# Second FFN of a macaron block: row normalization of the last blocks inside the mixer's pipeline, and row scatters issued in pairs that wait for the scatters ahead

## Chip, cores and metric

The kernel runs on one core of one Trainium2 chip. The metric is the device time of one launch in microseconds (us), lower is better. The engines are PE (TensorE, matmuls), DVE (VectorE), ACT (ScalarE), POOL (GpSimd) and SP (SyncE, which only issues DMAs here). Each engine runs its own list of instructions in order, and they wait for one another by semaphores.

## What is computed

The input x has 4 sequences of 1024 tokens with 128 features. Cut to its frame, the reference is

```python
x = x + 0.5 * ffn(layernorm(x))       # first FFN: shared + 2 of 8 experts per token
x = x + attn(layernorm(x))            # state space mixer with its own small FFN
x = x + 0.5 * ffn(layernorm(x))       # second FFN, same weights as the first

def ffn(x):
    shared = (silu(x @ sw1) * (x @ sw2)) @ sw3
    probs = softmax(x @ rw + rb); w, idx = top_k(probs, 2); w = w / sum(w)
    routed = sum over the 2 chosen experts e of w * ((silu(x @ ew1[e]) * (x @ ew2[e])) @ ew3[e])
    return shared + routed
```

## The kernel before

The 4096 tokens are 8 blocks (`NB`) of 512 tokens, each of 4 tiles of 128. The program has three phases: first FFN, mixer, second FFN. An FFN runs as follows for each block: statistics of x (`dve_stats`, L1374 and L1378), the power -0.5 of the variance on POOL (`pool_rstd`, L694 and L696), the normalized rows (`dve_norm`, L1390, four instructions), transposes on PE, router logits, the two chosen experts (`dve_route`, L1398 to L1420), a rank of every token within its expert (`pe_rank`, L1967 to L1971) and from it the row of a table in HBM where the token goes (`dve_places`, L1427 to L1437, whose last step increments `pos_ready`). `pool_scatter` (L703) then sends the rows of the block to the table `xs`: 8 indirect DMAs, one for each tile and each of the two chosen experts, each of 128 rows of 520 bytes. Each DMA adds 16 to the semaphore `scattered` when it has landed.

Beside the routing runs the shared FFN, two halves per block: `pe_up` (L1980 and L1982), silu on ACT (L1001), the product on DVE (`dve_hid`, L1474), `pe_down` (L1990) and the addition into x (`dve_shared`, L1479). Then SP loads tiles of 128 rows of one expert from `xs` (L458). It does so when all scatters have landed and when the last `pe_up` is done (L451), since the loads overwrite a buffer that `pe_up` reads. PE transposes these tiles (L2003), multiplies them with the expert's weights (L2016 to L2042), and POOL scatters the answers to `ys` (L719). At last DVE adds the answers to x (`dve_combine`, L1525).

The mixer is a software pipeline. `in_order` calls a body for n = -8 to 16, and each step in the body works on block n + k with a k of its own; the order of calls in the four bodies is the order of instructions on the engines. A block leaves the mixer with `ffn_add` (L1310, which increments `mixer_done`), and blocks 0 to 4 (`EARLY` = 5) go on in the same pipeline through the routing of the second FFN: `route_stats`, `route_rstd`, `route_rows`, `route_choice`, `route_places`, and the eight scatters of the block in four pairs (`route_scatter` 0 to 3). Blocks 5 to 7 are routed after the mixer, in `dve_ffn_again`, `pe_ffn_again` and `pool_ffn`. There DVE first takes the statistics and rows of the three blocks, then goes through the turns of the shared FFN with the routing of one late block in each of the first three turns. In the first FFN and after the mixer, POOL issues the 8 scatters of a block one behind the other with no wait between them.

Of the kernel before, what the change touches and what calls it, by code (L numbers as in the profile page):

```python
# [16 lines left out]
NB = TOK // BT  # L17
TT = BT // P
# [11 lines left out]
EARLY = 5  # L30
# [5 lines left out]
SQ = SEQ // BT  # L36
# [52 lines left out]
def macaron(nc, A, out):  # L89
    ctx = ExitStack()  # L90
    with ctx:
# [209 lines left out]
        scattered = sem("scattered")  # L301
# [80 lines left out]
        def do(work, block, *which):  # L382
            if block:
                work(*block, *which)

        def early(block):
            return block if block and SQ * block[0] + block[1] < EARLY else None

        def in_order(body):

            for n in range(-8, NB + 9):
                body(lambda k: (((n + k) // SQ, (n + k) % SQ) if 0 <= n + k < NB else None))
# [10 lines left out]
        block = ctx.enter_context(nc.Block())  # L403
# [101 lines left out]
        def pool_mixer(pool, ffn_own):  # L505
# [138 lines left out]
            def body(at):  # L644
# [3 lines left out]
                do(route_scatter, early(at(-9)), 0)  # L648
                do(route_rstd, early(at(-7)))
                do(route_scatter, early(at(-9)), 1)  # L650
# [47 lines left out]
        def pool_scatter(pool, turn, which=range(2 * TT)):  # L698

            n = turn % NB  # L700
            pool.wait_ge(pos_ready, turn + 1)
            for i in which:
                pool.indirect_dma_start(xs, bass.IndirectOffsetOnAxis(pos[:, n, i:i + 1], 0),  # L703
                                        rows[:, n * TT + i % TT, :], None).then_inc(scattered, 16)
# [18 lines left out]
        def pool_ffn(pool, own, call):  # L723
# [12 lines left out]
            else:  # L736

                for n in range(EARLY, NB):
                    pool_rstd(pool, own, NB + n)
                for n in range(EARLY, NB):  # L740
# [348 lines left out]
        def dve_mixer(dve, combine, ffn_own):  # L1089
# [238 lines left out]
            def body(at):  # L1328
                do(b_between, at(-4))
                do(route_stats, early(at(-7)))  # L1330
                do(ffn_hidden, at(-6), 0)
# [4 lines left out]
                do(stats_of, at(3))  # L1336
                do(route_rows, early(at(-7)))
                do(gram_copy, at(-4), 0)
# [240 lines left out]
        def dve_ffn_again(dve, own):  # L1579
            dve.wait_ge(mixer_done, NB)  # L1580
            late = range(EARLY, NB)
            for n in late:
                dve_stats(dve, own, NB + n)
            for n in late:
                dve_norm(dve, NB + n)
            for n in range(NB + 1):
# [5 lines left out]
                if n < NB:  # L1592
                    dve_hid(dve, NB + n, 1)
                if n:
                    dve_shared(dve, NB + n - 1)
# [590 lines left out]
```

## Time and profile before

| | us |
|---|---|
| median of 3 runs | 859.64 |
| lowest and highest run | 859.44, 863.35 |
| the profiled execution, own time | 859.07 |
| its span | 857.3 |
| share of the chain of waits put down to no engine of the profile | 15% |
| first FFN, to the first addition of its answers (L1525) | 0 to 266.9 |
| mixer, to the end of the last L1310 | 266.9 to 624.3 |
| second FFN, shared part and routing | 624.3 to 697.4 |
| second FFN, experts | 697.4 to 836 |
| last additions and stores | 836 to 857 |

A row of a timeline gives start, duration, engine, line, operation, output and inputs, how many instructions it merges, and in brackets the idle time of that engine just before and what ended it. The name "remote", and in the chain of waits "another core or an unknown queue", stands where the engine waited and the work on which it waited ended well before, so that the profile knows no releaser; there is only one core here.

### The profile page before, as it was taken

What the parts mean: (1) busy time and instruction counts of PE and PEld (TensorE: products, weight loads), DVE (VectorE), ACT (ScalarE), POOL (GpSimd) and SP (SyncE); (2) the same over time, 40 slices, a digit from 0 to 9 for tenths busy, and PEclk for the clock granted to TensorE, in tenths of its full rate; (3) what the DMA queues carried; (4) which work ended last, traced back from release to release, by engine and by line L of the source; (5) the groups of instructions that cost most, each with busy time, mean ns of one, the idle gap of its engine ahead of it and who ended that gap; (6) DMA issues with size and microseconds to landing.
All of it is one profiled execution on the core that took longest, in us unless ns stands there. A gap on an engine that the chain in (4) does not pass through costs nothing.

```text
span 857.3 us, 13671 instructions
## 1 busy us (share of the span) xinstructions
PE 659.9 (77%) x3768; PEld 481.7 (56%) x3768; DVE 543.7 (63%) x1730; ACT 413.1 (48%) x713; POOL 518.4 (60%) x656
## 2 busy tenths in 40 slices
PE   2448489888970557989999998989788689898840
PEld 2325258777760225656676665757555468686730
DVE  5535355544535787897999999997363445445518
ACT  1212124444430899997999998552121124344410
POOL 3875573555554675896978878767736105565550
PEclk9977889999995869889999998999979799999975
DMA  9311123222214100000000000000101122222218
GB/s 269 126 51 35 40 70 78 67 73 72 80 39 156 41 0 1 1 2 1 1 2 1 1 14 16 10 23 27 37 14 50 40 51 77 70 76 71 62 47 268
DMA packets 55512, 46.34 MB, mean 54 GB/s; under 512 B 8456, under 2 KB 51053, under 8 KB 55440
## 3 DMA queue, kind: packets, MB, share of 16 engines
q1 hardware_dynamic: 46736, 28.54, 12.2%
q0 software_dynamic: 8704, 16.93, 6.0%
q8 instruction: 34, 0.56, 0.3%
q14 instruction: 38, 0.31, 0.1%
HBM read 25.30 MB, written 21.19 MB: 54 GB/s over the span
## 4 chain that ended last, share of the span: by engine, by line
PE 42%; DVE 19%; another core or an unknown queue 15%; ACT 10%; issue 9%; POOL 3%; DMA 2%; DVEq 0%; POOLq 0%; ACTq 0%; SPq 0%
PE ps_tr L1640 3%; PE ps_tr L2042 3%; PE ps_go L2029 3%; PE ps_go L1640 2%; DVE x L1525 2%; PE ps_a L1980 2%; PE ps_b L1982 2%; PE ps_go L1990 2%; PE ps_go L2042 2%; PE ps_a L2018 2%; PE ps_go L1811 1%; PE ps_tr L1828 1%; ACT arena L1030 1%; PE ps_a L2016 1%
## 5 line engine op out<-in xcount | busy, mean ns | idle before, releaser
L719 POOL DMA_INDIRECT ys<-arena,dest x144 | 140.8, 978 | 154.5 <-DVE arena L1517 91.6
L703 POOL DMA_INDIRECT xs<-rows,pos x128 | 126.0, 984 | 67.7 <-issue 35.3
L2029 PE MATMUL ps_go<-ident,hid 128*128 128x128 f32 x288 | 44.3, 277 | 26.5 <-ACT arena L1030 18.0
L1001 ACT ACTIVATE silu_a<-ps_a 128x512 f32<-128x512 f32 x32 | 19.0, 597 | 94.3 <-remote 46.5
L2029 PEld LDWEIGHTS ps_go<-ident,hid 128*128 128x128 f32 x288 | 34.4, 142 | 41.8 <-issue 33.0
L1030 ACT ACTIVATE arena<-ps_go 128x512 f32<-128x512 f32 x72 | 43.0, 597 | 27.6 <-remote 21.8
L2042 PE MATMUL ps_tr<-w_down_e,arena 128*128 x384 | 52.4, 281 | 0.0
L1507 DVE TENSOR_TENSOR hid<-silu_a,ps_b 128x512 f32<-128x512 f32 x36 | 24.7, 685 | 38.6 <-issue 31.2
L2042 PEld LDWEIGHTS ps_tr<-w_down_e,arena 128*128 128x128 f32 x384 | 48.2, 197 | 0.0
L1990 PEld LDWEIGHTS ps_go<-w_shared_down,hid 128*128 128x128 f32 x256 | 34.7, 213 | 16.2 <-issue 16.0
L1507 DVE TENSOR_TENSOR hid<-silu_a,ps_a 128x512 f32<-128x512 f32 x36 | 24.6, 685 | 28.7 <-issue 16.3
L1021 ACT ACTIVATE silu_a<-ps_b 128x512 f32<-128x512 f32 x36 | 21.5, 598 | 43.0 <-remote 21.3
L1990 PE MATMUL ps_go<-w_shared_down,hid 128*128 128x128 f32 x256 | 35.1, 295 | 9.0 <-DVE x L1479 9.0
L1474 DVE TENSOR_TENSOR hid<-silu_a,ps_b 128x512 f32<-128x512 f32 x32 | 21.9, 686 | 29.9 <-PE ps_b L1982 15.7
L1517 DVE COPY arena<-ps_tr 128x256 f32<-128x256 f32 x48 | 20.3, 423 | 29.8 <-remote 24.4
L1479 DVE TENSOR_TENSOR x<-x,ps_go 128x512 f32<-128x512 f32 x16 | 11.0, 686 | 43.8 <-remote 30.3
L1811 PE MATMUL ps_go<-arena,state 128*128 128x128 f32 x128 | 32.2, 336 | 8.2 <-DVE us L1277 6.9
L1013 ACT ACTIVATE xt_hi<-ps_tr 128x256 fp32r<-128x256 f32 x48 | 18.5, 385 | 39.9 <-PE ps_tr L2003 25.6
L1021 ACT ACTIVATE silu_a<-ps_a 128x512 f32<-128x512 f32 x36 | 21.6, 600 | 32.9 <-PE ps_a L2018 18.0
L2016 PE MATMUL ps_a<-up_hi,xt_hi 128*128 x72 | 31.5, 438 | 5.2 <-DVE xt_lo L1492 3.8
L1941 PE MATMUL ps_tr<-ident,rows 128*128 128x128 f32 x64 | 14.0, 358 | 26.8 <-DVE rows L1390 19.8
L1811 PEld LDWEIGHTS ps_go<-arena,state 128*128 128x128 f32 x128 | 22.2, 207 | 20.4 <-issue 13.9
(366 smaller groups left out, 2053.0 us busy)
## 6 DMA issues: line engine op xcount, KB each, us to landing
arena<-xs SPq DMA_DIRECT2D x144, 65.0 KB
rows<-ys SPq DMA_DIRECT2D x8, 512.0 KB, 4.0
arena<-ys SPq DMA_DIRECT2D x8, 512.0 KB, 7.7
ys<-arena,dest POOLq DMA_INDIRECT x144
x<-in_L_attn_x SPq DMA_DIRECT2D x8, 256.0 KB, 4.4
arena<-in_L_ffn_ew SPq DMA_DIRECT2D x4, 512.0 KB, 6.3
xs<-rows,pos POOLq DMA_INDIRECT x128
out<-x SPq DMA_DIRECT2D x8, 256.0 KB, 3.8
```

The lines of the kernel that those rows point to most:

```text
L703: pool.indirect_dma_start(xs, bass.IndirectOffsetOnAxis(pos[:, n, i:i + 1], 0), rows[:, n * TT + i % TT, :], None).then_inc(scattered, 16)
L719: pool.indirect_dma_start(ys, bass.IndirectOffsetOnAxis(dest[:, i:i + 1], 0), y_out[:, p % YRING, j, :], None, bounds_check=2 * TOK - 1, o ...
L1021: act.activation(silu_a[:, p % 2, :].rearrange("p (j h) -> p j h", j=2), ps_pair[p % 2][:, :, 0:HID], ACT.Silu).then_inc(silu_e_done, 1)
L1030: act.activation(hid_t[:, p % 2, :], ps_d, ACT.Copy).then_inc(ht_ready, 1)
L1474: dve.tensor_tensor(hid[:, turn % 2, k, :], silu_a[:, k, :], ps_b[:, k, :], ALU.mult).then_inc(hid_done, 1)
L1507: dve.tensor_tensor(hid[:, p % 2, 0, :].rearrange("p (j h) -> p j h", j=2), silu_a[:, p % 2, :].rearrange("p (j h) -> p j h", j=2), ps_pai ...
L1640: r = pe.matmul(target, weights(k), zt[:, shift:shift + BT], start=(k == 0), stop=(k == taps - 1))
L1811: pe.matmul(pb["o"][:, at], state[:, k % 2, p * P:(p + 1) * P], cfs[:, q, k * P:(k + 1) * P], start=True, stop=False)
L1990: r = pe.matmul(ps_d[:, t * P:(t + 1) * P], hid[:, turn % 2, k, t * P:(t + 1) * P], w_shared_down[:, k, :], start=(k == 0), stop=(k == 1))
L2016: pe.matmul(target, xt_hi[:, p % 2, mine], hi, start=True, stop=False)
L2029: r = pe.transpose(ps_d[:, at:at + P], hid[:, p % 2, 0, at:at + P], ident[:, :])
L2042: r = pe.matmul(ps_answers(p)[:, j * P:(j + 1) * P], hid_t[:, p % 2, at:at + P], w_down_e[:, bass.ds(which[2 * p + j], 1), k, :].rearrange ...
```

## The change

Three things change in the second FFN, none in the first.

- `route_stats` and `route_rstd` in the mixer's pipeline are called for all 8 blocks, and `route_rows` for all but the last. The work for blocks 5 to 7 at the head of `dve_ffn_again` and `pool_ffn` is gone; the rows of block 7 are made after the two products of the first turn.
- `pool_scatter`, when it works for the second FFN (`turn >= NB`), waits before every second scatter until all scatters ahead have landed. This holds for the 40 scatters in the mixer's pipeline and for the 24 after it.
- Logits, choices, ranks and places of blocks 5 to 7 stay where they are.

```diff
@@ macaron
+        def not_last(block):
+            return block if block and SQ * block[0] + block[1] < NB - 1 else None
@@ pool_mixer, body
                 do(route_scatter, early(at(-9)), 0)
-                do(route_rstd, early(at(-7)))
+                do(route_rstd, at(-7))
                 do(route_scatter, early(at(-9)), 1)
@@ pool_scatter
             n = turn % NB
             pool.wait_ge(pos_ready, turn + 1)
             for i in which:
+                if turn >= NB and i % 2 == 0:
+                    pool.wait_ge(scattered, 16 * (turn * 2 * TT + i))
                 pool.indirect_dma_start(xs, bass.IndirectOffsetOnAxis(pos[:, n, i:i + 1], 0),
@@ pool_ffn
-                for n in range(EARLY, NB):
-                    pool_rstd(pool, own, NB + n)
                 for n in range(EARLY, NB):
                     pool_scatter(pool, NB + n)
@@ dve_mixer, body
-                do(route_stats, early(at(-7)))
+                do(route_stats, at(-7))
...
-                do(route_rows, early(at(-7)))
+                do(route_rows, not_last(at(-7)))
@@ dve_ffn_again
             dve.wait_ge(mixer_done, NB)
-            late = range(EARLY, NB)
-            for n in late:
-                dve_stats(dve, own, NB + n)
-            for n in late:
-                dve_norm(dve, NB + n)
...
                     dve_hid(dve, NB + n, 1)
+                if n == 0:
+                    dve_norm(dve, NB + NB - 1)
```

POOL at the end of the mixer's pipeline, from the addition of the last block's h to x. Before, where `scattered` is not waited for:

```order
L623 TENSOR_TENSOR x<-x,arena 128x512 [waits m_hmv]
...
L703 DMA xs<-rows,pos 33920x130 [waits pos_ready]
L703 DMA xs<-rows,pos 33920x130
L703 DMA xs<-rows,pos 33920x130 [waits pos_ready]
L703 DMA xs<-rows,pos 33920x130
L694 TENSOR_SCALAR var_eps<-mv 128x4 [waits mv_ready]
L696 TENSOR_TENSOR rstd<-var_eps,minus_half 128x4 [waits own_pool]
```

After, from the same instruction on:

```order
L626 TENSOR_TENSOR x<-x,arena 128x512 [waits m_hmv]
L709 DMA xs<-rows,pos 33920x130 [waits scattered,pos_ready]
L709 DMA xs<-rows,pos 33920x130
L709 DMA xs<-rows,pos 33920x130 [waits scattered,pos_ready]
L709 DMA xs<-rows,pos 33920x130
L709 DMA xs<-rows,pos 33920x130 [waits scattered,pos_ready]
L709 DMA xs<-rows,pos 33920x130
L697 TENSOR_SCALAR var_eps<-mv 128x4 [waits mv_ready]
L699 TENSOR_TENSOR rstd<-var_eps,minus_half 128x4 [waits own_pool]
L709 DMA xs<-rows,pos 33920x130 [waits scattered,pos_ready]
...
```

Before, six pairs stand in a row and the three L694/L696 of blocks 5 to 7 come behind them. Now the power for block 6 stands behind the third pair, that of block 7 behind the sixth (that of block 5 is between pairs one step earlier), and each pair waits for `scattered`.

DVE at the end of the mixer and the start of the second FFN. Before:

```order
L1304 TENSOR_TENSOR arena<-arena,ps_b 96x512 [waits m_silu_g,m_up_ps]
L1310 TENSOR_TENSOR x<-x,ps_tr 128x512 [waits m_h_added,m_ffn_ps]
L1374 BN_STATS stats<-x 128x6 [waits m_mixer_done]
...
L1390 TENSOR_SCALAR rows<-x,mv,rstd 128x128 [waits rstd_ready,mv_ready]
L1390 TENSOR_SCALAR rows<-x,mv,rstd 128x128 x3
L1474 TENSOR_TENSOR hid<-silu_a,ps_b 128x512 [waits down_ps_ready,b_ps_ready,silu_done] x2
L1398 TENSOR_TENSOR logits<-ps_tr,rb 128x32 [waits logits_ps_ready]
```

After:

```order
L1308 TENSOR_TENSOR arena<-arena,ps_b 96x512 [waits m_silu_g,m_up_ps]
L1394 TENSOR_SCALAR rows<-x,mv,rstd 128x128 [waits rstd_ready,mv_ready]
L1394 TENSOR_SCALAR rows<-x,mv,rstd 128x128 x3
L1314 TENSOR_TENSOR x<-x,ps_tr 128x512 [waits m_h_added,m_ffn_ps]
L1378 BN_STATS stats<-x 128x6 [waits m_mixer_done]
...
L1478 TENSOR_TENSOR hid<-silu_a,ps_b 128x512 [waits b_ps_ready,down_ps_ready,silu_done,m_mixer_done]
L1478 TENSOR_TENSOR hid<-silu_a,ps_b 128x512 [waits down_ps_ready,b_ps_ready,silu_done]
L1394 TENSOR_SCALAR rows<-x,mv,rstd 128x128 [waits rstd_ready,mv_ready]
L1394 TENSOR_SCALAR rows<-x,mv,rstd 128x128 x3
L1402 TENSOR_TENSOR logits<-ps_tr,rb 128x32 [waits logits_ps_ready]
```

The rows of block 6 now stand ahead of the last `ffn_add`, which lets PE start the second FFN. Twelve statistics and twelve row instructions ahead of the first product become four statistics, and the rows of block 7 stand between the second product and the first late choice.

## Rows read from the trace of the kernel before

**Rows 1.** Chain of waits, 580 to 700 us: start, length, what; the unknown pieces.

```profile
588.38 2.24 another core or an unknown queue
...
614.45 9.13 another core or an unknown queue
...
657.09 12.83 another core or an unknown queue
```

**Rows 2.** Timelines by engine, end of the mixer, 606 to 624 us.

```profile
606.50 1.07 POOL L703 DMA_INDIRECT xs<-rows,pos  x1 [0.17 <-issue]
...
620.51 0.96 POOL L703 DMA_INDIRECT xs<-rows,pos  x1 [0.30 <-issue]
...
615.15 2.94 PE L1875 MATMUL ps_tr<-w_down,arena 128*128 128x128 f32 x24 [0.78 <-issue]
...
623.61 0.69 DVE L1310 TENSOR_TENSOR x<-x,ps_tr 128x512 f32<-128x512 f32 x1 [8.51 <-remote]
```

**Rows 3.** Timeline, second FFN, 644 to 672 us.

```profile
644.60 0.24 PE L1971 MATMUL ps_go<-chosen,ones 128*128 128x8 bf16 x4
...
648.85 0.19 DVE L1427 TENSOR_TENSOR place<-ps_go,base 128x32 f32<-128x32 f32 x1 [3.89 <-remote]
...
656.95 2.69 PE L1990 MATMUL ps_go<-w_shared_down,hid 128*128 128x128 f32 x16
...
668.96 0.96 POOL L703 DMA_INDIRECT xs<-rows,pos  x1 [0.30 <-issue]
669.94 0.69 DVE L1479 TENSOR_TENSOR x<-x,ps_go 128x512 f32<-128x512 f32 x1 [12.85 <-remote]
```

**Rows 4.** Timelines, mixer: scatters in pairs, with PE and ACT beside them.

```profile
558.59 0.96 POOL L703 DMA_INDIRECT xs<-rows,pos  x1 [0.30 <-issue]
...
559.38 0.27 PE L1745 MATMUL ps_a<-ident,bf 128*128 128x128 f32 x1
...
559.69 0.49 ACT L913 ACTIVATE tm<-ps_a 128x384 f32<-128x384 f32 x1 [6.37 <-PE ps_b L1788]
...
561.39 1.00 POOL L703 DMA_INDIRECT xs<-rows,pos  x1 [0.17 <-issue]
```

**Rows 5.** DMA, 606 to 624 us: all queues that moved anything.

```profile
q0 software_dynamic: 384, 0.80, 13.5%
```

**Rows 6.** Timeline by engine: head of the second FFN, DVE, then POOL.

```profile
627.87 3.23 DVE L1390 TENSOR_SCALAR rows<-x,mv,rstd 128x128 f32<-128x128 f32 x12
631.01 0.68 DVE L1474 TENSOR_TENSOR hid<-silu_a,ps_b 128x512 f32<-128x512 f32 x1
...
637.60 0.17 DVE L1437 CAST pos<-pos_f 128x8 uint32<-128x8 f32 x1
...
626.03 1.04 POOL L696 TENSOR_TENSOR rstd<-var_eps,minus_half 128x4 f32<-128x4 f32 x1
...
638.06 1.10 POOL L703 DMA_INDIRECT xs<-rows,pos  x1 [8.19 <-DVE pos L1437]
```

**Rows 7.** Chain of waits: the last answer scatter, from its issue to its landing.

```profile
830.22 2.11 DMA ys<-arena,dest
```

**Rows 8.** SP's waits, and timeline 684 to 706 us.

```profile
SPq L451 <- PE ps_b L1982: 14.8, 1, 14.8
...
692.24 13.27 SPq L458 DMA_DIRECT2D arena<-xs  x16
...
697.47 0.44 PE L2003 MATMUL ps_tr<-ident,arena 128*128 128x128 f32 x2 [0.78 <-DVE x L1479]
```

**Rows 9.** Window: stretch, length, busy of PE, PEld, DVE, ACT, POOL, granted clock, DMA, GB/s.

```profile
621.00:624.00 3.00, 0.00 (x0) 0.00 (x0) 0.40 (x1) 0.00 (x0) 0.47 (x1) 0.50 0.07 22
```

**Rows 10.** Chain of waits: matmuls of the shared FFN.

```profile
629.03 1.71 PE ps_b L1982 x2
...
686.79 1.78 PE ps_go L1990 x16
...
690.29 0.86 PE ps_a L1980 x2
```

## The prediction

> **What bounds the kernel now.** I read the chain of waits first. Of 857.3 us it puts 15% down to no engine, and three of these pieces lie where the change works: 2.2 us at 588, 9.1 us at 614 and 12.8 us at 657 [rows 1]. The timelines of the engines say what stands there. At the end of the mixer PE ends its last `down` at 618.09 (615.15 + 2.94), but the DVE addition that needs only that starts at 623.61, 5.5 us late [rows 2]. In the second FFN a rank matmul ends at 644.84 and DVE uses it at 648.85, 4.0 us late. A `pe_down` ends at 659.64 and DVE uses it at 669.94, 10.3 us late, and all other work of the shared FFN queues up behind [rows 3]. A long idle time whose releaser had been done for long means that the news of PE's end came late, not that an engine was slow. So what else ran? In each case POOL was issuing scatters back to back: 12 of them from 606.50, one each 1.26 us (0.96 busy, 0.30 of issue), the last at 620.51 [rows 2], and 16 up to 668.96 [rows 3]. The engines wake up 1 to 3 us after the start of the last one. Where only two scatters stand together and POOL then does something else, nothing is late: with one running, PE ends at 559.65 and ACT starts at 559.69; the next pair starts 1.8 us after the last one's end [rows 4].
>
> My reading is that PE's increments of semaphores are held up while POOL scatters without a pause, and pass when it pauses. That is inferred from coincidence in time; the trace has no row for the path itself.
>
> The Trainium skill (Runtime: NRT & Kernel Launch, section on instruction fetch mechanics) names another thing that can stop several engines without a releaser: instructions are streamed in blocks of 16 KiB by DMA. By this, stalls would go with instruction packets and the change would not touch them. The trace speaks against it: from 606 to 624 us only the software queue moved anything, 384 packets [rows 5].
>
> **The waits in `pool_scatter`.** A pair takes 1.26 to 1.40 us from first to second start (0.96 + 0.30; the first after other work is 1.10 or 1.07 long [rows 2, 6]), then its landing, then the release of POOL. The landing of an indirect DMA has one clean row, 2.11 us from issue [rows 7]. A release is 0.29 us, from the end of the cast at 637.77 to the scatter at 638.06 [rows 6]. Together 3.66 to 3.80; I take 3.75 us for a pair, where it was 2.52. Between the end of the second and the next start POOL pauses 1.4 us, close to the 1.8 us that were enough in [rows 4]. In the steady mixer most pairs already stand farther apart, so the wait is met when POOL comes to it. At 588 one pair follows another and waits 1.1 us, behind it is a product for the last block that is needed later.
>
> **End of the mixer.** The power of block 5 (1.4 us: 1.04 [rows 6] and a short instruction ahead) and one wait push POOL's train of six pairs from 606.5 to about 607.2. Behind the third pair (607.2 + 2 x 3.75 + 1.40 + 0.96 = 617.1) stands the power of block 6, done at 618.4. DVE waits for it with the rows of block 6 (3.23 / 3 = 1.1 us [rows 6]) **ahead of the last `ffn_add`**, which is thus free at 619.6. That is a new wait, but without the hold `ffn_add` could start at 618.1 at best. Against 623.61 the mixer ends 4.0 us earlier. The three remaining pairs run behind that, to about 628, and the power of block 7 comes at 629.6.
>
> **Head of the second FFN.** Removed in front of the first product are 8 of 12 statistics and all 12 row instructions. This looks like 6 us, but PE's `ps_b` for that product ended at 630.74 [rows 10] and DVE took it at 631.01 [rows 6], so the removal is worth 0.3 us. What is added is the rows of block 7 (1.1 us) between the second product and the choice of block 5. Places and scatters of block 5 move by -4.0 + 1.1: the first late scatter goes from 638.06 to 635.2.
>
> **Shared FFN.** From the rank matmul at 644.84 on, PE still has 11 halves of up (2 x 0.86 = 1.72) and 7 downs (1.78 [rows 10]), 31.4 us. I add 3 us for transposes and logits and 2.5 us for waits on DVE, both estimates: an end at 681.7 without any hold, where the trace has 697.4 with the last addition. Moved by -2.9 it is 678.8.
>
> **Scatters after the mixer.** Twelve pairs: 635.2 + 11 x 3.75 + 1.26 + 2.11 = 679.8. Before, this end was of no matter, since SP waited 14.8 us for the last up of PE [rows 8]. Now it is the later of the two, by a microsecond against the end of the shared FFN, by 6 against the last up. SP starts loading tiles at 679.9 instead of 692.24.
>
> **Start of the experts.** Before, PE started on the tiles 5.2 us after SP, held by the last addition. Now it is the loads themselves: 2.1 us of landing as in [rows 7] at least, 5.2 at most; I take 2.9, hence 682.8 instead of 697.47, 14.7 us earlier. Something is given back. PE is idle from about 678 on, and after such a stop the clock was granted at half (0.50 in 621 to 624, PE having stopped at 618 [rows 9]), the level of 1.2 GHz; two ups still took 1.71 us at 629 where they take 0.86 [rows 10]. That can cost 0 to 3.5 us of the experts; I take 2.5. The experts and the last additions are otherwise unchanged.
>
> **Sum.** Against the profiled execution of 859.07: -14.7 + 2.5 = -12.2, so 846.9. The median of the runs is 0.57 above it: 847.4 us.
>
> **Rivals.**
>
> - *Hold only in part gone.* A post may still be late within a pair. At some 0.4 us on each of three handoffs in eight turns, the shared FFN ends 10 us later (689) and binds again: 697.4 - 689 = 8.4 earlier, 851. A pair cadence of 4.2 us, with the fills of SP on the same DMA engines, gives 11 x 0.45 = 5 us later, 852. For it: the pause is shorter than in [rows 4]. Chance 0.20.
> - *No link.* The engines stall for another reason and as long as before, and the waits only make POOL's train longer. Then `ffn_add` and the end of the shared FFN stay, and the last landing (638.06 + 1.1 + 44.7 = 683.9) is before SP's 692.2: about 860. The Trainium skill (DMA: Bandwidth & Descriptors, rules for kernel authors) advises to issue DMAs early and wait late, since the fixed cost then overlaps, and this change does the reverse. By that rule alone it could not gain, and would come out here. Against it: every long stall lies on a train of scatters. Chance 0.07.
> - *Slower: the hold lasts for the train, pauses or not.* If 1.4 us are too little, posts wait until the train ends. The mixer's train ends near 630 instead of 623.6 (+6.4), and the late one, begun 7.5 us later, lasts 44.7 us to 690.3 where it ended near 671. Everything behind moves by 19 us: 878. It decides at the pause that a post needs, which is above 0 and, by [rows 4], at most 1.8. Chance 0.08.
> - *Main case*, 843 to 850. Chance 0.60. The last 0.05 is faster than that: both trains shorter (3.66 us a pair) and no loss of clock, down to 842.
> - That the edit does not do what it says is excluded by the order of instructions.
>
> **How the numbers follow.** The forecast is 847.4. The range 842 to 858 holds the main case with its bounds (cadence -1 to +0.6 us, load 2.1 to 5.2, clock 0 to 3.5) and the partial hold; it leaves out the two last rivals and a little more. A measurement can tell 0.5%, 4.3 us, from no change. Faster by more than that: 0.78. Within: 0.10. Slower: 0.12. Of the partial hold 0.13 counts as faster, 0.03 as within and 0.04, a hold of a larger size than the one priced, as slower.
>
> **What would show it.** Right: the last `ffn_add` starts within 0.2 us of the rows of block 6, near 619.6; no idle time of "remote" over 2 us until the tiles; scatters in pairs 3.7 us apart; SP's wait before the first tile ends with a landing, not with PE; a dip of the clock at the first tiles. Wrong: an idle time of DVE or ACT that still ends with the last scatter of a train; SP still waiting for PE; POOL's train so late that the power of block 7 holds the choice of block 5.

## The result

The changed kernel takes 853.2 us against 859.3 us (medians of 20 runs each), a ratio of 0.9942 with a 95% interval of 0.9919 to 0.9964. Faster, as forecast, but by 0.6% and not by the 1.4% that 847.4 us would have been: half of the gain did not come. One profiled execution of it has a span of 854.3 us, where the kernel before had 857.3.

The pieces without a releaser [rows 1] are gone between 480 and 700 us. What stands there in the chain of waits of the changed kernel (start, length, what) is POOL and the landings of its pairs:

```profile
by line: DMA xs<-rows,pos 45.9%; POOL xs L709 17.1%; issue 12.5%; DMA arena<-xs 4.8%; PE ps_a L2017 2.7%; SPq L461 2.0%; PE ps_a L2018 1.9%; PE ps_a L2019 1.9%; PE ps_b L2017 1.9%; PE ps_go L2004 1.6%; DVE hid L1478 1.5%; DVE top_i L1411 1.
...
612.87 2.28 DMA xs<-rows,pos
...
615.19 0.73 issue
615.92 0.96 POOL xs L709
...
661.56 0.27 issue
661.83 0.96 POOL xs L709
662.79 0.30 issue
663.09 3.02 DMA xs<-rows,pos
...
683.59 3.74 DMA xs<-rows,pos
...
691.34 0.35 SPq L461
```

(The first line has the shares of the stretch 655 to 700 us alone.) The timelines of the same kernel, answering to [rows 2], [rows 6] and [rows 8]: PE's last `down`, the rows of block 6 and the last `ffn_add`, the rows of block 7, the first late scatter, the last addition of the shared FFN, and PE's first tile.

```profile
617.86 2.94 PE L1876 MATMUL ps_tr<-w_down,arena 128*128 128x128 f32 x24 [0.78 <-DVE arena L1308]
...
624.00 1.12 DVE L1394 TENSOR_SCALAR rows<-x,mv,rstd 128x128 f32<-128x128 f32 x4 [6.20 <-POOL rstd L699]
625.03 0.68 DVE L1314 TENSOR_TENSOR x<-x,ps_tr 128x512 f32<-128x512 f32 x1
...
637.09 1.12 DVE L1394 TENSOR_SCALAR rows<-x,mv,rstd 128x128 f32<-128x128 f32 x4 [1.72 <-POOL rstd L699]
...
641.89 1.09 POOL L709 DMA_INDIRECT xs<-rows,pos  x1 [4.90 <-DVE pos L1441]
...
686.15 0.69 DVE L1483 TENSOR_TENSOR x<-x,ps_go 128x512 f32<-128x512 f32 x1 [2.21 <-PE ps_go L1991]
...
693.29 1.01 PE L2004 MATMUL ps_tr<-ident,arena 128*128 128x128 f32 x2 [7.17 <-DMA arena<-xs]
```

These times have to be read with a shift. One `hid` product of the mixer, long before anything that the change touches, starts at 472.04 in the kernel before and at 476.76 in the changed one:

```profile
472.04 1.76 DVE hid L1164
```

```profile
476.76 1.77 DVE hid L1168
```

So this execution of the changed kernel was 4.7 us late when the changed part began. With 4.7 us taken off, its first tile comes at 688.6 where it was at 697.47 [rows 8]: 8.9 us earlier, of a forecast 14.7.

### The profile page after: what moved, and what is told of

It reads as the page before. It is cut to its first block, busy times and chain, and to the rows that moved or that the text cites. A ratio compares the mean times of both kernels' runs of the same rounds, so it can differ in the third digit from the quotient of the medians.

```text
span 854.3 us, 13695 instructions
## 1 busy us (share of the span) xinstructions
PE 655.6 (77%) x3768; PEld 476.1 (56%) x3768; DVE 544.2 (64%) x1730; ACT 413.7 (48%) x713; POOL 519.3 (61%) x656
## 4 chain that ended last, share of the span: by engine, by line
PE 35%; another core or an unknown queue 14%; DVE 14%; issue 13%; ACT 9%; POOL 7%; DMA 6%; SPq 0%; POOLq 0%; DVEq 0%; ACTq 0%
DMA xs<-rows,pos 4%; POOL xs L709 4%; PE ps_tr L1641 4%; PE ps_go L1641 3%; PE ps_tr L2043 2%; PE ps_go L2030 2%; DVE x L1529 2%; ACT arena L1034 2%; PE ps_a L2019 2%; PE ps_go L1812 1%; PE ps_go L1816 1%; PE ps_go L1991 1%; PE ps_tr L1829 1%; PE ps_a L1981 1%
## 5 line engine op out<-in xcount | busy, mean ns | idle before, releaser
L1991 PEld LDWEIGHTS ps_go<-w_shared_down,hid 128*128 128x128 f32 x256 | 30.9, 193 | 7.2 <-issue 7.2
L2017 PE MATMUL ps_b<-up_hi,xt_hi 128*128 x72 | 32.2, 447 | 1.1 <-DVE xt_lo L1496 0.9
L1991 PE MATMUL ps_go<-w_shared_down,hid 128*128 128x128 f32 x256 | 31.5, 276 | 1.7 <-DVE x L1483 1.7
```

The source lines that it names most:

```text
L1991: r = pe.matmul(ps_d[:, t * P:(t + 1) * P], hid[:, turn % 2, k, t * P:(t + 1) * P], w_shared_down[:, k, :], start=(k == 0), stop=(k == 1))
L2017: pe.matmul(target, xt_hi[:, p % 2, mine], hi, start=True, stop=False)
```

## Experiments: two kinds of sessions

One thing must be told first. The kernels ran in several sessions (the texts written ahead of each run say "call"), each with runs of the kernel before on the same chip. In some sessions the median of the kernel before is 852 to 859 us, as in the first comparison; in others it is 781.8 to 782.7. Nothing lies between. y_before shows what is different.

**y_before** is the kernel before, unchanged.

> The kernel before, unchanged, for its trace beside the next ones. In the runs of the first comparison it took 859 us and its chain held pieces without a releaser; in the runs of moves-only and its three companions it took 783, and their traces have no such piece over 1.5 us although POOL scatters 12 and 24 in a row. Theory 'place' (whether the hold occurs depends on the chip or the process, not on the kernel): either some 782 us with no such piece, or some 859 with them, nothing in between. Rival 'luck within a run': a time between, with some of the pieces.

It took 782.1 us. By engine, the chain of its page has no unknown piece at all, where the kernel before had 15% in the first comparison. In the timelines, the last of twelve scatters starts at 584.60, and `ffn_add` follows the last `down` (end 582.20) without delay though the tenth is running; 24 late scatters run in a row up to 625.37, and the additions of the shared FFN are on time.

```profile
PE 49%; POOL 17%; DVE 13%; issue 10%; ACT 7%; DMA 2%; POOLq 0%; SPq 0%; DVEq 0%; ACTq 0%
```

```profile
579.26 2.94 PE L1875 MATMUL ps_tr<-w_down,arena 128*128 128x128 f32 x24 [0.78 <-DVE arena L1304]
...
582.24 0.69 DVE L1310 TENSOR_TENSOR x<-x,ps_tr 128x512 f32<-128x512 f32 x1 [3.04 <-PE ps_tr L1875]
...
584.60 0.96 POOL L703 DMA_INDIRECT xs<-rows,pos  x1 [0.30 <-issue]
...
595.77 1.10 POOL L703 DMA_INDIRECT xs<-rows,pos  x1 [6.09 <-DVE pos L1437]
...
640.83 0.44 PE L2003 MATMUL ps_tr<-ident,arena 128*128 128x128 f32 x2 [0.78 <-DVE x L1479]
```

So the hold, that is, news of PE's end that comes late while POOL scatters, is not a property of the kernel. It needs the scatters and something else that some sessions have. The chip's number does not tell it: sessions with the hold had the numbers 2, 3, 6, 8 and 14, those without 0, 6 and 8. What it is stays open. The loading of instructions does not explain it: both traces of the kernel before have the same 34 and 38 packets on the two instruction queues, and none of them moved from 640 to 650 us, where news was held.

Of the 77 us between the two traces of the kernel before, 42.3 lie before the first late scatter, and 35.6 of these before the mixer's first scatter (491.74 against 456.10), where the change does nothing. The part from the first late scatter to the first tile has 14.3 (59.4 against 45.1), the experts and what follows them 20.2 (159.8 against 139.6). So the change works on the smaller part of what the hold costs.

All comparisons, each against the kernel before in its own session, with the 95% interval:

| kernel | no hold | with the hold |
|---|---|---|
| changed kernel | 1.0173 (1.0144 to 1.0203) | 0.9942 (0.9919 to 0.9964) |
| moves only | 0.9976 (0.9959 to 0.9994), 0.9977 (0.9961 to 0.9993), 0.9989 (0.9974 to 1.0005) | 0.9947 (0.9906 to 0.9988) |
| waits only | 1.0230 (1.0200 to 1.0260) | |
| waits after the mixer only | 1.0068 (1.0045 to 1.0090) | |
| one wait a pair | | 0.9931 (0.9897 to 0.9965) |
| one wait, power first | 1.0306 (1.0262 to 1.0349) | |
| short pause, no wait | 0.9973 (0.9949 to 0.9996), 0.9960 (0.9938 to 0.9983) | 0.9938 (0.9898 to 0.9979) |
| fours | 1.0017 (0.9999 to 1.0034), 1.0027 (1.0012 to 1.0042) | |
| eights after the mixer | | 0.9836 (0.9810 to 0.9862) |
| fours after the mixer | | **0.9744** (0.9653 to 0.9835), **0.9784** (0.9742 to 0.9827) |

## Experiments: the parts of the change

**y_after** is the changed kernel, unchanged.

> The changed kernel, unchanged. Theory 'place': if the kernel before takes 859 us here, 853; if it takes 783 us, there is no hold to cure and only the price of the waits is left. Waits after the mixer alone were 788.8 (ratio 1.0068); with the pairs of 4.3 us in the mixer and the powers behind them the first late scatter comes some 4 to 5 us later still: 792 to 796 us, ratio 1.012 to 1.017, a slower kernel. Rival: the change is worth its 6 us everywhere, ratio 0.992 to 0.996.

795.1 us, ratio 1.0173: where there is no hold the change costs 1.7%, at the upper end of what "place" gave.

**x_moves_only, w_moves_only, v_moves_only, u_moves_only**, the changed kernel without the waits:

```diff
             for i in which:
-                if turn >= NB and i % 2 == 0:
-
-                    pool.wait_ge(scattered, 16 * (turn * 2 * TT + i))
                 pool.indirect_dma_start(xs, bass.IndirectOffsetOnAxis(pos[:, n, i:i + 1], 0),
```

> The changed kernel without the waits of the scatter pairs: only the statistics, powers and rows of blocks 5 to 7 are moved into the mixer's pipeline, and POOL scatters back to back as before. Theory 'hold' (PE's increments are late while POOL scatters without a pause, and the waits cure it): the idle pieces without a releaser come back at the end of the mixer (some 5 us between the end of the last down and the last ffn_add) and in the second FFN (4 and 10 us or more), SP again waits for the last up and not for a landing, and the time is that of before, 857 to 861 us (ratio to before 0.998 to 1.002). Rival 'moves' (the gain of 6 us comes from the moved rows): 852 to 854 us, ratio 0.992 to 0.995, with the stalls in place.

> The kernel of x_moves_only again (the moved statistics, powers and rows, without any wait for landings), for a call in which the hold shows. Where it does not, this kernel was 1.9 us faster than the kernel before (0.9976), while the changed kernel was 1.7% slower. Theory 'hold': the pieces without a releaser stand at the mixer's end and in the second FFN as in the kernel before, ratio 0.996 to 1.002. Rival 'the moves bring the gain': 0.990 to 0.995, no slower than the changed kernel.

> The kernel of x_moves_only once more; the question is what it does where the hold shows (kernel before some 855 to 860 us). Theory 'hold': its chain of waits has again pieces without a releaser of several us in the mixer's end and in the second FFN, and its ratio is 0.996 to 1.002, against 0.9942 of the changed kernel. Rival 'the moves bring the gain': 0.990 to 0.995. If the call falls where the kernel before takes 782 us: 0.9976 for the third time.

> The kernel of the moves-only runs once more, for a call in which the hold shows. v_pause_short fell into such a call: no piece without a releaser at the mixer's end, where the moved powers part the scatters into groups of six, but three in the second FFN (1.6, 1.9 and 10.6 us) that end 2.1 us after the last of 16 scatters. Theory 'a train of more than some six scatters holds until it has landed': without any pause the same: nothing or under 2 us at the mixer's end, 8 to 15 us in the second FFN, ratio 0.992 to 0.998. Rival 'the short pauses did it at the mixer's end': 5 us late there as in the kernel before, ratio 0.998 to 1.002.

The first three fell where there is no hold and gave 781.3, 781.0 and 780.8 us: the moved rows are worth 1 to 2 us by themselves there, and the waits cost 1.9%, some 14 us (795.1 against 781). The fourth had the hold, and my main theory, that the waits bring the gain, fell with it: 0.9947 (0.9906 to 0.9988), within the intervals as good as the changed kernel, without one wait. Its timeline shows two different things. At the end of the mixer nothing is late any more: the last `down` ends at 621.13 and `ffn_add` starts at 621.36, though twelve scatters run there as before. They are now six, the power of block 6, and six. In the second FFN the hold is there as before. The rank matmul ends at 642.03, 0.4 us into the sixth scatter, and DVE uses it at 645.15; ACT wakes at 646.58, after the eighth, and DVE again after the next eight.

```profile
618.19 2.94 PE L1873 MATMUL ps_tr<-w_down,arena 128*128 128x128 f32 x24 [0.78 <-DVE arena L1305]
...
617.84 0.95 POOL L706 DMA_INDIRECT xs<-rows,pos  x1 [0.31 <-issue]
618.82 0.27 POOL L697 TENSOR_SCALAR var_eps<-mv 128x4 f32<-128x4 f32 x1
619.17 1.04 POOL L699 TENSOR_TENSOR rstd<-var_eps,minus_half 128x4 f32<-128x4 f32 x1
620.41 1.09 POOL L706 DMA_INDIRECT xs<-rows,pos  x1 [0.20 <-issue]
...
621.36 0.68 DVE L1311 TENSOR_TENSOR x<-x,ps_tr 128x512 f32<-128x512 f32 x1
...
641.79 0.24 PE L1969 MATMUL ps_go<-chosen,ones 128*128 128x8 bf16 x4
...
644.18 0.96 POOL L706 DMA_INDIRECT xs<-rows,pos  x1 [0.30 <-issue]
...
645.15 0.19 DVE L1428 TENSOR_TENSOR place<-ps_go,base 128x32 f32<-128x32 f32 x1 [3.00 <-issue]
...
646.58 0.60 ACT L1002 ACTIVATE silu_a<-ps_a 128x512 f32<-128x512 f32 x1 [4.93 <-remote]
...
655.18 0.95 POOL L706 DMA_INDIRECT xs<-rows,pos  x1 [0.30 <-issue]
...
658.00 0.69 DVE L1480 TENSOR_TENSOR x<-x,ps_go 128x512 f32<-128x512 f32 x1 [9.95 <-remote]
```

**x_waits_only**, the kernel before plus those waits alone.

```diff
             for i in which:
+                if turn >= NB and i % 2 == 0:
+                    pool.wait_ge(scattered, 16 * (turn * 2 * TT + i))
                 pool.indirect_dma_start(xs, bass.IndirectOffsetOnAxis(pos[:, n, i:i + 1], 0),
```

> The kernel before plus only the waits of the scatter pairs; statistics, powers and rows of blocks 5 to 7 stay after the mixer. Theory 'hold': no idle piece without a releaser over 2 us, but the three powers now stand behind a POOL train that ends near 632 (six pairs of 4.3 us from 606.5), so that the rows and with them the first late scatter come near 646 where the changed kernel (its first 480 us being those of before) has 637. The late train of 49 us follows: some 5 to 9 us later than the changed kernel, 857 to 862 us. Rival 'waits alone bring it, moves are neutral': 852 to 854 us.

No hold in its session, and 802.7 us, 20 more than the kernel before. The reason is the one given: the three powers stand behind a train whose last scatter starts at 594.29 (584.60 in y_before), and the first late scatter starts at 609.76 after POOL has waited 10.4 us for DVE, where y_before has 595.77.

```profile
594.29 0.96 POOL L706 DMA_INDIRECT xs<-rows,pos  x1 [0.30 <-issue]
...
598.32 1.05 POOL L696 TENSOR_TENSOR rstd<-var_eps,minus_half 128x4 f32<-128x4 f32 x1
609.76 1.10 POOL L706 DMA_INDIRECT xs<-rows,pos  x1 [10.38 <-DVE pos L1440]
```

**x_waits_late**, the changed kernel with waits after the mixer only.

```diff
-                if turn >= NB and i % 2 == 0:
+                if turn >= NB + EARLY and i % 2 == 0:
```

> The changed kernel with the waits only in turns 13 to 15, that is for the twelve pairs after the mixer; the pairs in the mixer run without. Theory 'hold, each train for itself': the last ffn_add is again 5 us late behind the mixer's train, but the powers of blocks 6 and 7 no longer stand behind pairs of 4.3 us, which costs the changed kernel 2 us before the first late scatter and some more of the mixer's end. Together 0 to 3 us slower than the changed kernel: 853 to 856 us, ratio to before 0.993 to 0.997. Rival 'the gain is made in the mixer': near 859 us.

788.8 us without the hold. That splits the price of 14 us in two: 7.5 for the pairs after the mixer (788.8 against 781.3), 6.3 for those in it (795.1 against 788.8, in two sessions whose kernel before differs by 0.5).

## Experiments: what a pair costs

**z_one_wait** keeps the wait for a block's positions only where it is needed.

```diff
-            pool.wait_ge(pos_ready, turn + 1)
+            if which[0] == 0:
+                pool.wait_ge(pos_ready, turn + 1)
```

> The changed kernel with one edit: in the mixer the wait for a block's positions stands only ahead of its first pair, so that seven of eight pairs there have a single wait, the one for the landing. Expected from the trace of the changed kernel (0.73 us from a passed wait to the start where there are two, 0.27 where there is one): the pairs of the mixer's end 3.8 instead of 4.32 us apart. Two of them stand ahead of the power of block 6 and four ahead of that of block 7, so the rows of block 7 and with them everything behind come 1.5 to 2.5 us earlier: where the kernel before takes 782 us, 792.5 to 794 against 795.1 of the changed one (ratio 1.012 to 1.015 against 1.0173); where it takes 859, 851 (0.990 to 0.993 against 0.9942). Rival: the 0.46 us are a matter of the profile and nothing changes, 1.0173 or 0.9942.

This was the first of these sessions with the hold: 847.7 us, ratio 0.9931. It lies where it was expected, but its interval also holds the 0.9942 of the changed kernel, so the time settles nothing. The trace does: the pairs behind the power of block 6 stand 3.81 us apart (619.78 to 623.59), not 4.3, and the rows of block 7 start without waiting for POOL.

```profile
619.78 0.96 POOL L710 DMA_INDIRECT xs<-rows,pos  x1 [1.59 <-DMA xs<-rows,pos]
...
623.59 0.96 POOL L710 DMA_INDIRECT xs<-rows,pos  x1 [1.58 <-DMA xs<-rows,pos]
```

**y_one_wait_rstd** adds a second edit.

```diff
-                do(route_scatter, early(at(-9)), 0)
                 do(route_rstd, at(-7))
+                do(route_scatter, early(at(-9)), 0)
                 do(route_scatter, early(at(-9)), 1)
```

> The changed kernel with two edits in POOL's mixer program: the power of a block goes ahead of the first pair of the turn instead of behind it, and the wait for a block's positions stands only ahead of its first pair. Reason for the second: in the trace of the changed kernel a pair with both waits starts 0.73 us after its wait has passed, one with a single wait 0.27, so pairs in the mixer take 4.32 and not 3.81 us. Expected: the power of block 6 some 5.8 us earlier (one pair and three times 0.5), the last ffn_add 3 to 4 us earlier, and the first late scatter 4 to 5 us earlier, since rows of block 7 no longer wait for POOL. End 3 to 5 us below the changed kernel, whether or not the hold is there. If the mixer's end is set by something else: within 1 us of it.

A miss: 805.3 us, ten more than the changed kernel. I had looked at the mixer's end only. In the steady mixer the power waits for DVE's statistics (5.02 us at 504.35), and now a pair and all of POOL's mixer work stand behind that wait. The first late scatter comes at 609.58 where y_after has 600.33.

```profile
504.35 0.23 POOL L697 TENSOR_SCALAR var_eps<-mv 128x4 f32<-128x4 f32 x1 [5.02 <-DVE mv L1383]
504.67 1.04 POOL L699 TENSOR_TENSOR rstd<-var_eps,minus_half 128x4 f32<-128x4 f32 x1
505.90 1.11 POOL L710 DMA_INDIRECT xs<-rows,pos  x1 [0.20 <-issue]
```

## Experiments: what ends the hold

**y_pause_short, w_pause_short, v_pause_short** have a small memset on POOL after every pair in place of the wait.

```diff
-                if turn >= NB and i % 2 == 0:
-                    pool.wait_ge(scattered, 16 * (turn * 2 * TT + i))
                 pool.indirect_dma_start(xs, bass.IndirectOffsetOnAxis(pos[:, n, i:i + 1], 0),
+                if turn >= NB and i % 2 == 1:
+                    if rests[0]:
+                        pool.wait_ge(rest_done, rests[0])
+                    pool.memset(rest[:, :], 0.0).then_inc(rest_done, 1)
+                    rests[0] += 1
```

> The changed kernel with, in place of each wait for a landing, a memset of 128 x 128 bf16 on POOL after every second scatter (0.22 to 0.28 us by the memsets of that size in the trace of before, and some issue time around it). Any number of scatters may then be in flight, and a pair takes some 2.9 us instead of 3.81. Where the kernel before takes 859: theory 'a pause of the issue is enough' gives 844 to 849, since the late train of 12 pairs ends some 10 us earlier and the shared FFN binds; rival 'the landing is what matters' gives 856 to 862 with the pieces back. Where it takes 783 neither shows, and the time is 781 to 784.

> The kernel of y_pause_short again, for a call in which the kernel before takes some 855 to 860 us and shows the pieces without a releaser (y_pause_short fell where it takes 782; there a pair took 2.9 us and the kernel 780.5). Theory 'a pause of the issue is enough', that is, it is the back-to-back issue that holds the news and not the number in flight: 840 to 848 us, ratio 0.980 to 0.989, no piece over 2 us in the mixer's end and the second FFN. Rival 'what counts is that the scatters have landed': 853 to 860 us, ratio 0.995 to 1.002, with the pieces back. If the call falls where the kernel before takes 782: 780.5 again.

> The kernel of the two short-pause runs once more, for a call in which the hold shows (kernel before some 855 to 860 us). Theory 'a pause of the issue is enough': pairs 2.9 us apart with any number of scatters in flight, and no piece without a releaser over 2 us in the mixer's end and the second FFN: ratio 0.980 to 0.989. Rival 'what counts is that the scatters have landed': 0.995 to 1.002, with the pieces back. Where the kernel before takes 782 us: 0.996 to 0.997 again.

Pairs are 2.6 to 2.75 us apart. Without the hold the kernel takes 780.5 and 778.4 us, as moves only or a little less. With it, 848.7 us (0.9938, interval 0.9898 to 0.9979): between my two numbers, since the first theory wanted 0.980 to 0.989 and the second 0.995 to 1.002. The trace speaks against the first in the second FFN. PE ends a `pe_down` at 639.45, and DVE uses it at 650.56, 2.1 us after the end of the sixteenth scatter, although POOL had paused 0.2 to 0.4 us after each pair. By the trace, what was gained came from the mixer's end, where nothing is late, as in u_moves_only.

```profile
637.50 1.95 PE L1996 MATMUL ps_go<-w_shared_down,hid 128*128 128x128 f32 x16
...
647.48 0.96 POOL L709 DMA_INDIRECT xs<-rows,pos  x1 [0.30 <-issue]
648.44 0.22 POOL L714 MEMSET rest<- 128x128 bf16 x1
...
650.56 0.69 DVE L1488 TENSOR_TENSOR x<-x,ps_go 128x512 f32<-128x512 f32 x1 [10.65 <-remote]
```

**x_fours, w_fours** wait ahead of every fourth scatter.

```diff
-                if turn >= NB and i % 2 == 0:
+                if turn >= NB and i % 4 == 0:
```

> The changed kernel with a wait for the landing ahead of every fourth scatter instead of every second. A group of four takes 4 x 1.26 + 2.28 + 0.27 - 1.26 = 6.3 us where two pairs take 7.6 (trace of the changed kernel: 1.26 to the next start, 2.28 from the last start to its landing, 0.27 release), so the late train of 24 scatters lasts some 41 instead of 49 us. Theory 'a pause every fourth is enough': holds of at most 2 us each, the tiles start 5 to 8 us earlier, 846 to 850 us. Rival 'two in a row are the most that passes': each group holds PE's news for 3 to 5 us, the shared FFN binds again, 854 to 860 us.

> The kernel of x_fours again (a wait for the landing ahead of every fourth scatter), for a call in which the hold shows. Its late train takes some 42 us (603 to 638 and a landing in the trace of x_fours) where that of pairs takes 49. Theory 'a pause every fourth is enough': 846 to 850 us, ratio 0.985 to 0.990. Rival 'the news of a group of four comes only at its end': each handoff of PE to DVE and ACT in the shared FFN is up to 3.8 us late, the end of the shared FFN binds again: 853 to 860 us, ratio 0.994 to 1.001. Where the hold does not show: 784 against 782 us again.

Both fell where there is no hold: 784.2 us twice, 3 us over moves only. Of the 14 us that pairs cost, fours cost 3. On the hold they say nothing.

**t_fours_late, s_fours_late** put the two findings together: the moved powers part the train in the mixer, and after it a landing is waited for ahead of every fourth scatter.

```diff
-                if turn >= NB and i % 2 == 0:
+                if turn >= NB + EARLY and i % 4 == 0:
```

> The changed kernel with waits for the landing only after the mixer and only ahead of every fourth scatter. For a call in which the hold shows. There u_moves_only (no waits) had no piece without a releaser at the mixer's end, one of 1.2 and one of 9.9 us in the second FFN, and PE's first tile at 694.1; in x_fours the late train from its first scatter to SP's start on the tiles took 41.4 us. From the first late scatter of u_moves_only, 635.2, SP would start at 676.6 and PE at 678.6, 15.5 earlier; a slower clock gives 3 back. Theory 'landed every fourth is enough': ratio 0.979 to 0.984, 837 to 842 us, no piece over 2 us. Rival 'four in a row already hold': pieces of 2 to 4 us within each group, PE's last up late again, ratio 0.990 to 0.998. Where the kernel before takes 782 us: between 781 and 784.

> The kernel of t_fours_late again, for a narrower interval where the hold shows or for its price where it does not. With the hold: ratio 0.970 to 0.980. Without (kernel before 782 us): x_fours, with waits in the mixer too, was 784.2, the moved rows alone 781; the waits after the mixer make SP start on the tiles 2 us later than there (677 against 634.8 of x_moves_only counted from its own first late scatter: 41 us of train against 39.9 to the end of the last up), so 781.5 to 783.5 us, ratio 0.998 to 1.001: no loss.

830.9 us (0.9744, below the 0.979 to 0.984 expected, with an interval that reaches into it) and, in another session, 840.1 us (0.9784, inside the expected range; kernel before 858.2): 2.2 to 2.6% below the kernel before and, by the ratios of different sessions, some 1.6 to 2% below the changed one. In the first trace `ffn_add` follows `down` at once, no piece without a releaser over 1 us stands between the mixer's end and the first tile, which comes at 681.91 and is again released by the shared FFN's last addition, and the clock of PE does not drop in this stretch.

```profile
624.10 0.69 DVE L1314 TENSOR_TENSOR x<-x,ps_tr 128x512 f32<-128x512 f32 x1 [0.97 <-PE ps_tr L1876]
...
642.73 0.95 POOL L709 DMA_INDIRECT xs<-rows,pos  x1 [1.58 <-DMA xs<-rows,pos]
...
681.91 0.44 PE L2004 MATMUL ps_tr<-ident,arena 128*128 128x128 f32 x2 [0.78 <-DVE x L1483]
```

```profile
620.00:700.00 80.00, 71.98 (x418) 52.08 (x418) 44.12 (x160) 25.18 (x48) 37.60 (x41) 1.00 0.19 54
```

**s_eights_late** waits only ahead of each of the three late blocks, in the same session as s_fours_late.

```diff
-                if turn >= NB and i % 2 == 0:
+                if turn >= NB + EARLY and i == 0:
```

> The changed kernel with a wait for the landing only ahead of the first scatter of each of the three blocks after the mixer. In u_moves_only the first eight late scatters run from 635.21 to 644.18 without a pause, and ACT's 4.9 us without a releaser end at 646.58, 2.4 us after the start of the eighth: the hold ends with the landing, and eight are enough for it. Theory 'eight hold, four do not': with the hold, each block has a piece of 3 to 6 us, ratio 0.984 to 0.992, worse than s_fours_late by 1% at least. Rival 'any landed pause is as good': ratio as s_fours_late within 0.3%. Where the kernel before takes 782 us: 780 to 782.

844.4 us (0.9836), slower than fours in the same session by 0.5%, half of the 1% expected, and the two intervals overlap a little; by time alone the order of the two is likely, not settled. In the trace two of the three trains of eight hold the news, by 4.7 us (PE's end at 638.89) and 2.3 us (653.94), and it comes about when the eighth has landed: last start 641.05, DVE wakes at 643.59.

```profile
641.05 0.96 POOL L709 DMA_INDIRECT xs<-rows,pos  x1 [0.31 <-issue]
...
643.59 0.19 DVE L1431 TENSOR_TENSOR place<-ps_go,base 128x32 f32<-128x32 f32 x1 [4.59 <-remote]
...
656.21 0.69 DVE L1483 TENSOR_TENSOR x<-x,ps_go 128x512 f32<-128x512 f32 x1 [4.92 <-remote]
```

The Trainium skill (Perfetto Trace Analysis, DMA Instruction — SWDGE (GPSIMD)) says that the end of such an instruction in a profile is the end of writing its descriptors, not of moving the data. The trace of u_moves_only agrees: the scatter of 617.84 ends at 618.79, and the DMA engines are busy again (share 0.65) from 619.3 to 619.6.

What ends the hold is not settled. For the landing speak the wake-ups 2.4 to 3.1 us after the last start in three traces with groups of eight and sixteen, where a landing takes 2.28 from there, and [rows 2]. Against it: in [rows 3] and at 645.15 in u_moves_only DVE wakes 1.0 us after the last start, and in v_pause_short news passes in the middle of a train (DVE at 636.27, after 1.6 us, with the eighth scatter still to come). And no run separates a landing from a pause of POOL. In the mixer's end of u_moves_only the next group starts 2.57 us after the start of the sixth scatter, and in [rows 4] the next pair 2.8 us after that of the second: by 2.28 us these had landed too, with no wait for it.

Nor is it settled how many scatters it takes; a count alone does not set it. At the mixer's end of the kernel before, a matmul that ended at 614.38, with the seventh scatter running, reached DVE at 614.41. In the second FFN of four traces, news was held from the sixth scatter on. And in a train of four in the mixer, from 584.88 to 588.78, PE's end at 588.93 reached DVE 1.7 us late, which is the first piece of [rows 1]; the same stands in s_eights_late (590.19, and 591.85). There two instruction packets moved near by, so this one may have another cause. A train of four in u_moves_only, up to 593.44, held nothing.

```profile
588.33 0.60 PE L1788 MATMUL ps_b<-tm 128*128 128x256 f32 x2
...
590.64 0.48 DVE L1262 SCALAR_TENSOR_TENSOR state_new<-ps_b,decay,own_head 128x256 f32<-128x256 f32 x1 [2.27 <-remote]
```

## Why the prediction was right in sign and wrong in size

*The hold* was read rightly from the trace of before: where it shows at all, it is bound to scatters in a row, and with landed pairs it is gone. That a pause of 1.4 to 1.8 us is enough held for these pairs, and at the mixer's end of u_moves_only without a wait; whether it is the pause or the landing within it, no run tells.

*The end of the mixer* is where the credit went to the wrong part. I let the waits bring 4.0 us and only charged the power of block 6 to the moves. The moves alone do it, most likely because the power splits the train (they also reorder DVE's work there): with them `ffn_add` is 0.2 us behind the last `down`. With the waits it is 4.2 us behind (620.80 to 625.03), held by the rows of block 6. So at this place the waits cost 4 us that the changed kernel could have had. The forecast of 619.6 is met by accident, 620.3 with the shift taken off.

*The cadence of a pair*, 3.75 us from bounds of 3.66 and 3.80, was the step that failed most. In the mixer's end it is 4.3 to 4.5 us. Two rows explain it: from a passed landing POOL needs 0.73 us where two waits stand ahead of the scatter, 0.27 where there is one. My release of 0.29 came from a scatter with one wait [rows 6], and the code has two in each call from the mixer. Three such pairs, and then three more, stand ahead of the power of block 7, for which DVE waits 1.7 us. In the five of them that follow another pair or a power this is 2.3 us, more than the 1.7, and the 1.7 is nearly all of the 2.0 us by which the first late scatter is late (637.2 with the shift off, forecast 635.2). After the mixer a pair takes 3.81 us at best, 4.56 where it waits for DVE's positions (658.01), 4.55 beside the fills of SP (663.09, landing after 3.02) and 5.27 once (683.59, landing after 3.74). The landing that I took had nothing beside it [rows 7]; 2.28 is the usual one here. The Trainium skill (DMA: Bandwidth & Descriptors, Anatomy of one DMA — SWDGE (gpsimd) path) gives 2.0 us plus the bytes by 436 GB/s, an estimated 2.15 for these 65 KB, which is as near as [rows 7] and would not have saved the forecast.

*The late train* is the sum of this: from its first scatter to SP's first tile it takes 49.4 us where the forecast has 44.7, and SP waits for it and not for PE. I saw that the train and the shared FFN would be within a microsecond and called the train's end the later one, but took its bounds from single rows without company; the last landing (691.15) is 4.3 us behind the last addition (686.84). That addition is 3.3 us later than forecast itself (682.1 with the shift off, for 678.8), 2.0 of them from the first late scatter, but nothing waits for it.

In a row, for the profiled executions and against the forecast: first late scatter +2.0, train +4.7, SP to PE -0.95 (1.95 for 2.9), together the 5.8 us between the forecast first tile (682.8) and 688.6. The clock gives back 3.1 for a forecast 2.5: PE was idle 7.2 us, the clock is at the lower of its two levels in the first 8 us of the tiles (0.51, 1.2 GHz), and from the first tile to the first `ident` product it takes 7.7 us instead of 4.6.

```profile
693.00:701.00 8.00, 7.31 (x19) 5.10 (x20) 2.65 (x10) 1.64 (x4) 0.00 (x0) 0.51 0.41 91
701.00:709.00 8.00, 8.00 (x54) 7.07 (x53) 4.93 (x14) 4.30 (x9) 2.24 (x3) 1.00 0.27 69
```

Then -8.9 + 3.1 = -5.8 us is what the change did in these executions, and the medians say -6.2. The rest of the difference between the two spans is not the change's: +4.7 before it begins and -1.9 in the experts, whose code is the same, where holds of 2 to 3 us come and go.

*The rivals.* "Hold only in part gone" had the right time (852, from a cadence of 4.2 us) and its second half the right mechanism; its first half did not happen. "No link" is wrong where I forecast, but right wherever the hold does not show: there the waits only lengthen POOL's train (795.1 against 781 us), as by the rule of the Trainium skill (DMA: Bandwidth & Descriptors, Rules for kernel authors) to issue a DMA early and wait for it late. Its 860 was too kind, since I let SP's old wait for PE hide the train; it does not when PE is not held. I had no case in which the hold itself depends on the session, and nothing in one trace could have told me. And I never asked for a variant with fewer waits, though the price of each stood in my own sum.

Left open: what makes the hold show in some sessions; at how many scatters it begins; whether a landing or a longer pause ends it; what the waits alone, and those after the mixer alone, are worth with the hold, since both ran only without it; and fours after the mixer where there is no hold, which did not run (x_fours, with waits in the mixer too, costs 0.2 to 0.3% there, so it should cost no more). The answer scatters of the experts, with 20 us between the two kinds of sessions, were not touched.

## What to carry to other kernels

When a wait cures a stall, price both in the same stage: here a landing ahead of each pair cost 14 us where there was no stall, and with the stall gained nothing over the moves alone (0.9942 and 0.9947). One ahead of every fourth cost a fifth of that, and after the mixer it kept the cure. Ask of each part of a change what it does alone; a short piece of other work in the middle of a train of scatters did at the mixer's end what the waits did, for nothing. And put a wait that is nearly always met on the first of a group only: a second wait ahead of the same instruction costs time each time that the first one is really waited for.

## What the runs showed of the hardware

- Whether PE's news is late while POOL scatters in a row depends on the session: 859 or 782 us for the same kernel, with chips of the same numbers in both groups. News of ACT and DVE was not seen late.
- Where it is so, groups of four with a landing between them, after the mixer, were free of it (t_fours_late, s_fours_late), and so were two groups of six 1.6 us apart at the mixer's end (u_moves_only); two of three groups of eight held news by 4.7 and 2.3 us (s_eights_late), in the first of them from the sixth scatter on; pauses of 0.2 to 0.4 us after each pair did not end it.
- A scatter behind one passed wait starts 0.27 us after it, behind two 0.73.
- A landing takes 2.28 us from the start of a scatter of 128 rows of 520 bytes. Beside eight fills of 65 KB it took 3.02 in one trace (663.09) and 4.52 in another (z_one_wait, 653.74), and once 3.74 without them.
